# A phase mixer and a ternary FFN on one core: VectorE and ScalarE get new orders, and all steps are written out

## Chip, core and metric

The kernel runs on one core of one Trainium2 chip. The metric is device time in microseconds (us), from one execution's start to its end; the median of several runs counts, lower is better. One further execution was recorded by the hardware profiler.

## The reference

The input x has 16 sequences of 1024 positions of 256 features, all float32. The layer adds two blocks to it, each behind a layer norm:

```python
x = x + mixer(layernorm(x)); x = x + ffn(layernorm(x))
# mixer(x):
phi = cumsum((x @ W_omega.T + b_omega) * exp(log_scale) / sqrt(position), axis=1)
cm_real, cm_imag = x * cos(phi), x * sin(phi)
mem_real, mem_imag = cumsum(cm_real) / position, cumsum(cm_imag) / position
ret_real = mem_real * cos(phi) + mem_imag * sin(phi)
ret_imag = mem_imag * cos(phi) - mem_real * sin(phi)
context = concatenate([cm_real, cm_imag, ret_real, ret_imag])          # 1024 wide
return x + gelu(layernorm(context) @ W1.T + b1) @ W2.T + b2            # 1024 -> 512 -> 256
# ffn(x): weights rounded to -1, 0, 1:
return relu(x @ Wq1.T + b1) @ Wq2.T + b2                               # 256 -> 1024 -> 256
```

## The kernel before

The 16,384 positions are cut into 32 chunks of 512, two to a sequence; a chunk's second half of the state (the running sums of phase and memory) comes from the chunk ahead of it in the same sequence. Inside, features lie on the 128 partitions: a tile of [128, 2, 512] is one chunk of 256 features, called a wide tile here; a half-wide one is [128, 512]. To keep float32 accuracy in float16 matmuls, each activation is split: ScalarE casts the high part (`ch`, `gh`, `rh`, `xh`), and VectorE subtracts it from the whole for the low part (`cl`, `gl`, `rl`, `xl`).

The work is a software pipeline written by hand. Each engine has a function `step(s)`, which lists its operations for several chunks at once: `now` (chunk s, in its FFN), `nxt` (s+1, in the mixer's W1, Gelu and W2), `ahead` (s+2, in sine, cosine, running sums and retrieval), `far` (s+3, in the first norm and the phases). Engines run their lists strictly in order, and meet at semaphores: `need(engine, semaphore, chunk)` waits until that chunk's operation is done, and the last argument of `then_inc` names what an operation reports.

TensorE's step (not changed) is: `hidden` 0 and 1 (24 matmuls each, line 817), the statistics of the context (790, 796), `hidden` 2, `spread` of the context's reciprocal deviation `crs` (803), `hidden` 3, then `ffn_in` 0 to 7 (832) with the bias rows (842) and `ffn_out` (848) three blocks behind, `mixer_out` (864, 867), `omega` (777) and the last three `ffn_out`. `ffn_out(m)` needs `relu_lo(m)` of VectorE; `ffn_in(m)` for m below 4 needs the PSUM bank that `scale_hidden(m)` frees; `ffn_in(0)` needs the transposed rows that SyncE's DMAs bring after `second_lo`.

VectorE (`dve`) does `scale_hidden` (line 1160), `memory_real` and `memory_imag` (1099, 1105, times 1/position), the scans (1054, 1078, 1086), `relu_lo` (1204), `gelu_lo` (1165), `context_lo` (1136), `second_lo` (1196), `mixer_residual` (1172), `phase_turns` (1046), `output` (1210) and the small norm statistics. ScalarE (`act`) does all casts and tables. GpSimd (`pool`), whose list is not changed, does in each step: `inverse_std_2`, `square_lo`, `inverse_std_1`, `inverse_std_context` (474, writes `crs`), `product_imag_sin` (509, writes `qa`) and `square_sums` (494 and 496). `square_sums` waits for `square_real`, for `square_imag` and for `context_lo` of part 3:

```python
                need(pool, sqr_done, c)
                need(pool, sqi_done, c)
                need(pool, cl_done[3], c)
                pool.tensor_tensor(sqr[:, :, :], sqr[:, :, :], turn[:, :, :], ALU.add).then_inc(q2_done, 1)
```

Steps -1 to 1 and 28 to 31 are written out; steps 2 to 27 run as a hardware loop of 13 turns with two steps each, on every engine.

## Time and profile before

| | us |
|---|---|
| median of 3 runs | 1623.66 (1623.33 to 1623.72) |
| profiled execution, its own time | 1623.21 |
| its span, first to last instruction | 1621.1 |
| TensorE busy / VectorE busy | 1530.3 / 1470.2 |
| ScalarE busy / GpSimd busy | 1241.1 / 348.0 |

The granted TensorE clock is 0.987 of full speed on average and full over the steady steps. Busy time is time in which an engine executes something; on TensorE the ends of matmuls are modelled, and neighbours overlap, so starts are the better reading there. On VectorE and ScalarE too an instruction starts up to 0.1 us before its predecessor's end. In the rows below PE is TensorE, DVE VectorE, ACT ScalarE, POOL GpSimd, SPq SyncE's queue; "idle before <-releaser" is the time an engine stood still ahead of the instruction and who let it go.

### The profile page before, as it was taken

The page shows a single profiled execution, that of the slowest core. Times are in us where ns is not written, and L with a number is a line of the kernel's source. Part 1 is how long each engine was busy: PE and PEld are TensorE (multiplying, and loading weights), DVE is VectorE, ACT ScalarE, POOL GpSimd, SP SyncE. Part 2 cuts the span into 40 slices and gives each one's busy share as a digit, 9 for nine tenths or more (in the row PEclk, how much of TensorE's full clock was granted, in tenths as well). Part 3 has the DMA queues.
Part 4 walks back from the last instruction along what each step waited for, and adds up shares of the span by engine and source line. Part 5 has one row for each costly group of instructions (what it writes and reads, how often), then busy time and mean ns, then how long its engine had stood idle before and what let it go on. Part 6 is the DMA issues. An engine that isn't in the chain of part 4 may idle for free.

```text
span 1621.1 us, 31250 instructions
## 1 busy us (share of the span) xinstructions
PE 1530.3 (94%) x11177; PEld 925.6 (57%) x11177; DVE 1470.2 (91%) x2448; ACT 1241.1 (77%) x1773; POOL 348.0 (21%) x235
## 2 busy tenths in 40 slices
PE   3689999999999999999999999999999999999995
PEld 2455556566555665655566565556665555656553
DVE  7999999999999999999999999999999999999843
ACT  6678877787887787787777788777778777877843
POOL 1221222121122212212222211222221222222110
PEclk9899999999999999999999999999999999999998
DMA  5001111100111101111110111111001111010011
GB/s 201 14 14 27 40 40 40 36 16 26 39 39 39 39 24 28 26 39 39 39 39 13 26 39 39 39 39 36 16 26 39 39 39 39 23 28 15 27 27 39
DMA packets 109079, 57.95 MB, mean 36 GB/s; under 512 B 73456, under 2 KB 107504, under 8 KB 109040
## 3 DMA queue, kind: packets, MB, share of 16 engines
q1 hardware_dynamic: 107408, 53.77, 11.7%
q10 hardware_dynamic: 1632, 3.67, 0.6%
q8 instruction: 23, 0.38, 0.1%
q14 instruction: 16, 0.13, 0.0%
HBM read 23.87 MB, written 16.78 MB: 25 GB/s over the span
## 4 chain that ended last, share of the span: by engine, by line
DVE 42%; ACT 26%; issue 24%; PE 3%; POOL 3%; DVEq 1%; ACTq 1%; DMA 0%; SPq 0%; POOLq 0%
ACT arena L624 8%; ACT arena L599 6%; DVE ph L1054 5%; DVE mr L1086 5%; DVE mi L1078 4%; ACT arena L633 4%; DVE arena L1136 4%; DVE ph L1046 3%; DVE bn L1179 2%; DVE cmi L1071 2%; DVE xl L1038 2%; DVE rows L1196 2%; DVE x L1172 2%; DVE cmr L1069 2%; ACT xf L614 2%
## 5 line engine op out<-in xcount | busy, mean ns | idle before, releaser
L817 PE MATMUL ps<-arena,w_hi 128*128 128x512 f16 x2048 | 609.0, 379 | 2.9 <-DVE arena L1136 1.7
L817 PE MATMUL ps<-arena,w_lo 128*128 128x512 f16 x1024 | 388.0, 379 | 0.0
L817 PEld LDWEIGHTS ps<-arena,w_hi 128*128 128x128 f16 x2048 | 197.8, 98 | 223.7 <-issue 2.1
L848 PE MATMUL ps<-fw_t,arena 128*128 128x256 f16 x2048 | 254.6, 272 | 17.0 <-DVE arena L1204 16.0
L832 PE MATMUL ps<-turned,fw_t 128*128 128x512 f16 x1024 | 253.5, 381 | 13.0 <-DMA turned<-rows 13.0
L848 PEld LDWEIGHTS ps<-fw_t,arena 128*128 128x128 f16 x2048 | 191.5, 97 | 92.9 <-issue 58.0
L494 POOL TENSOR_TENSOR sqr<-sqr,turn 128x1024 f32<-128x1024 f32 x32 | 75.4, 2357 | 677.5 <-DVE arena L1136 677.5
L1204 DVE TENSOR_TENSOR arena<-arena 128x512 f16<-128x512 f32 x256 | 172.2, 683 | 41.6 <-ACT arena L633 41.4
L624 ACT ACTIVATE arena<-ps,relu_bias,relu_scale 128x512 f32<-128x512 f32 x256 | 194.1, 770 | 13.4 <-PE ps L832 13.3
L867 PE MATMUL ps<-w_hi,arena 128*128 128x256 f16 x1024 | 183.4, 273 | 0.0
L817 PEld LDWEIGHTS ps<-arena,w_lo 128*128 128x128 f16 x1024 | 100.1, 98 | 120.9
L585 ACT CAST sqr<-sqr 128x512 f16<-128x512 f32 x32 | 19.8, 618 | 188.4 <-POOL sqr L496 188.4
L832 PEld LDWEIGHTS ps<-turned,fw_t 128*128 128x128 f16 x1024 | 100.5, 98 | 101.3 <-DMA turned<-rows 13.3
L633 ACT CAST arena<-arena 128x512 f16<-128x512 f32 x256 | 153.3, 611 | 0.0
L867 PE MATMUL ps<-w_lo,arena 128*128 128x256 f16 x512 | 139.6, 273 | 0.0
L599 ACT ACTIVATE arena<-arena,b_full,z_down 128x512 f32<-128x512 f32 x128 | 103.5, 809 | 27.3 <-DVE arena L1160 27.3
L867 PEld LDWEIGHTS ps<-w_hi,arena 128*128 128x128 f16 x1024 | 100.2, 98 | 11.6
L509 POOL TENSOR_TENSOR qa<-mi,sn 128x1024 f32<-128x1024 f32 x32 | 76.5, 2390 | 100.7 <-DVE mi L1105 100.7
L603 ACT ACTIVATE arena<-arena,up 128x512 f16<-128x512 f32 x128 | 92.5, 722 | 4.2
L1165 DVE SCALAR_TENSOR_TENSOR arena<-arena,up 128x512 f16<-128x512 f32 x128 | 92.2, 741 | 0.0
L1160 DVE TENSOR_TENSOR arena<-ps,rb 128x512 f32<-128x512 f32 x128 | 81.8, 680 | 8.8 <-ACT rb L595 5.5
L474 POOL TENSOR_TENSOR crs<-cve,minus_half 128x4 f32<-128x4 f32 x32 | 33.3, 1040 | 228.0 <-DVE cve L1153 228.0
(190 smaller groups left out, 2739.7 us busy)
## 6 DMA issues: line engine op xcount, KB each, us to landing
x_rows<-in_L_attn_x SPq DMA_DIRECT2D x32, 512.0 KB, 3.5
out<-x SPq DMA_DIRECT2D x32, 512.0 KB, 2.9
arena<-in_L_attn_W ACTq DMA_DIRECT2D x1, 2048.0 KB, 11.2
arena<-in_L_ffn_W SPq DMA_DIRECT2D x2, 1024.0 KB, 10.4
turned<-rows SPq DMA_TRANSPOSE x128, 2.4
arena<-in_L_attn_ln_gamma ACTq DMA_DIRECT2D x1, 512.0 KB, 6.5
pos_rsqrt<-in_positions SPq DMA_DIRECT2D x1, 512.0 KB, 15.1
arena<-in_L_attn_ln_beta ACTq DMA_DIRECT2D x1, 512.0 KB, 12.7
```

Source lines behind the costliest of these rows:

```text
L599: act.activation(z[:, m], z[:, m], ACT.Gelu, scale=z_down[:, 0:1], bias=b1_full[:, m:m + 1])\
L603: act.activation(gh[:, m], z[:, m], ACT.Copy, scale=up[:, 3:4]).then_inc(gh_done[m], 1)
L624: act.activation(rf[:, m % SLOTS], ps[:, 4 + m % KE], ACT.Relu, scale=relu_scale[:, 0:1], bias=relu_bias[:, m:m + 1]).then_inc(relu_done[m ...
L633: act.copy(rh[:, m % SLOTS], rf[:, m % SLOTS]).then_inc(rh_done[m % SLOTS], 1)
L817: last = pe.matmul(ps[:, 4 + m], w[:, k, m * P:(m + 1) * P], a[:, c.b, k], start=(i == 0), stop=(i == len(passes) - 1))
L832: last = pe.matmul(ps[:, 4 + m % KE], fw1_t[:, k, m * P:(m + 1) * P], a[:, k], start=(i == 0), stop=(i == len(passes) - 1))
L848: last = pe.matmul(ps_rows_a[:, j], a[:, m % SLOTS, j * P:(j + 1) * P], fw2_t[:, m], start=False, stop=(m == KF - 1 and a is rl), skip_gro ...
L867: last = pe.matmul(ps_rows_b[:, j], a[:, m, j * P:(j + 1) * P], w[:, m], start=False, stop=(i == len(passes) - 1))
L1054: last = dve.tensor_tensor_scan(ph[:, k], ones[:, 0:1].to_broadcast([P, CH]), ph[:, k], ph_carry[:, k] if c.b else 0.0, ALU.mult, ALU.add)
L1160: dve.tensor_tensor(z[:, m], ps[:, 4 + m], rb[:, :], ALU.mult).then_inc(z_done[m], 1)
L1165: dve.scalar_tensor_tensor(out=gl[:, m], in0=z[:, m], scalar=up[:, 3:4], in1=gh[:, m], op0=ALU.mult, op1=ALU.subtract).then_inc(gl_done[m], 1)
L1204: dve.tensor_tensor(rl[:, m % SLOTS], rf[:, m % SLOTS], rh[:, m % SLOTS], ALU.subtract)\
```

## The change

Two things change. The loop is gone: `run` now lists all 33 steps on every engine. And the lists of VectorE and ScalarE are in a new order, for which some helper functions are cut in two (`sin_cos` into `sine` and `cosine`, `modulate` into its parts, `gelu` and `first_out` into a function and its cast); the carries of the running sums are copied only in a sequence's first chunk. `phase_sums` stands at the end of a step for `far` where it stood at the start of the next for `ahead`. The lists of TensorE, GpSimd and SyncE keep their order. The diff, cut to its core:

```diff
-            for s in range(first, LOOP_FROM):
-                step(Step(Counts(eng, s - s % 2), s % 2))
-            with eng.Fori(LOOP_FROM // 2, LOOP_TO // 2) as pair:
-                counts = Counts(eng, pair * 2)
-                step(Step(counts, 0))
-                step(Step(counts, 1))
-            for s in range(LOOP_TO, CHUNKS):
+            for s in range(first, CHUNKS):
                 step(Step(Counts(eng, s - s % 2), s % 2))
...
 
             def step(s):
                 now, nxt, ahead, far = s.chunk(0), s.chunk(1), s.chunk(2), s.chunk(3)
+                if nxt:
+                    sums_hi(nxt)
                 if ahead:
-                    act.activation(idle_sine[:, :], half_pi[:, 0:1], ACT.Sin)
                     whole_turns(ahead)
+                    base_scaled(ahead)
+                    sine(ahead)
                 if now:
                     normalise_2(now)
                 if ahead:
-                    sin_cos(ahead)
+                    cosine(ahead)
...
@@ -650,40 +652,63 @@
                 if now:
                     second_hi(now)
                 if ahead:
-                    base_scaled(ahead)
+                    context_hi(ahead, 1, cmi_done, cmi[:, :, :])
                     context_hi(ahead, 0, cmr_done, cmr[:, :, :])
...
                 if nxt:
                     spread_out(nxt)
                     gelu(nxt, 0)
                     gelu(nxt, 1)
...
-                    if m == 6 and ahead:
-                        square_imag(ahead)
-                if now:
-                    relu_hi(now, KF - 1)
+                if now:
+                    relu_hi(now, 0)
+                    relu(now, 1)
+                    relu(now, 2)
+                    relu_hi(now, 1)
+                    relu_hi(now, 2)
+                if nxt and now:
+                    gelu(nxt, 3)
+                if now:
+                    relu(now, 3)
+                    relu_hi(now, 3)
+                if nxt and now:
+                    gelu_hi(nxt, 3)
+                if now:
+                    relu(now, 4)
+                    relu(now, 5)
+                    relu_hi(now, 4)
+                if far:
+                    first_turned(far)
+                if now:
+                    relu_hi(now, 5)
+                    relu(now, 6)
+                if far:
+                    first_hi(far)
+                if now:
+                    relu(now, 7)
                 if ahead:
+                    square_imag(ahead)
                     context_hi(ahead, 2, rr_done, rr[:, :, :])
                     context_hi(ahead, 3, ri_done, ri[:, :, :])
-                    sums_hi(ahead)
+                if now:
+                    relu_hi(now, 6)
+                    relu_hi(now, 7)
+                if ahead:
+                    square_real(ahead)
+                if far:
+                    act.activation(idle_sine[:, :], half_pi[:, 0:1], ACT.Sin)
 
...
-            def carries(c):
-                need(dve, sumi_done, c)
-                dve.tensor_copy(mi_carry[:, :, :], mi[:, :, CH - 1:CH]).then_inc(icarry_done, 1)
+                if not c.b:
+                    need(dve, sumr_done, c)
+                    dve.tensor_copy(mr_carry[:, :, :], mr[:, :, CH - 1:CH]).then_inc(rcarry_done, 2)
+
...
             def step(s):
                 before, now, nxt, ahead, far = s.chunk(-1), s.chunk(0), s.chunk(1), s.chunk(2), s.chunk(3)
-                if ahead:
-                    phase_sums(ahead)
                 if now:
                     lean_2(now)
                 if before:
@@ -1226,63 +1263,73 @@
                     bias_pieces()
                     dve.wait_ge(p_fw1, 16)
                     signs(0, fw1_in, fw1_signs)
+                if ahead:
+                    modulate_imag(ahead)
+                    sums_imag(ahead)
+                    modulate_real(ahead)
+                    memory_imag(ahead)
                 if far:
                     gains_1(far)
-                if ahead:
-                    modulate(ahead)
-                if now:
-                    second_lo(now)
-                if ahead:
-                    sums_imag(ahead)
                 if nxt:
                     context_variance(nxt)
                 if far:
                     unit_squares(far)
+                if now:
+                    second_lo(now)
                 if ahead:
                     sums_real(ahead)
-                    carries(ahead)
-                    memory_imag(ahead)
                 if nxt:
...
                 if ahead:
                     memory_real(ahead)
+                    retrieve_imag_cos(ahead)
+                    retrieve_real_cos(ahead)
                 if nxt:
                     scale_hidden(nxt, 3)
-                if ahead:
-                    retrieve_real_cos(ahead)
-                    retrieve_imag_cos(ahead)
-                    product_real_sin(ahead)
...
                 if ahead:
+                    retrieve(ahead)
+                if now:
+                    relu_lo(now, 0)
+                if ahead:
+                    product_real_sin(ahead)
+                if now:
+                    relu_lo(now, 1)
+                    relu_lo(now, 2)
+                if nxt and now:
+                    gelu_lo(nxt, 0)
+                if ahead:
+                    context_lo(ahead, 0, cmr[:, :, :])
+                if nxt and now:
+                    gelu_lo(nxt, 1)
+                if now:
+                    relu_lo(now, 3)
+                if nxt and now:
+                    gelu_lo(nxt, 2)
+                if now:
+                    relu_lo(now, 4)
+                if nxt and now:
+                    gelu_lo(nxt, 3)
+                if ahead:
+                    retrieve_imag(ahead)
+                if now:
+                    relu_lo(now, 5)
+                if far:
+                    first_lo(far)
+                if ahead:
+                    context_lo(ahead, 1, cmi[:, :, :])
                     context_lo(ahead, 2, rr[:, :, :])
                     context_lo(ahead, 3, ri[:, :, :])
+                if now:
+                    relu_lo(now, 6)
+                    relu_lo(now, 7)
                 if nxt and not now:
                     dve.wait_ge(p_turned, FW1_TURNED)
                 if nxt:
@@ -1292,6 +1339,8 @@
                 if nxt:
                     statistics_2(nxt)
                     spread_2(nxt)
+                if far:
+                    phase_sums(far)
 
```

VectorE around the variance of the context, first before, then in the changed kernel: from `cve`, the last row of the variance, on. `sq` belongs to `unit_squares`, `rows` is `second_lo`, `arena<-ps,rb` is `scale_hidden`.

```order
L1153 TENSOR_SCALAR cve<-cvar 128x4
L1030 SCALAR_TENSOR_TENSOR sq<-rs,mv 128x4
L1033 TENSOR_TENSOR sq<-sq,rs 128x4
L1086 SCALAR_TENSOR_TENSOR mr<-ones,mr_carry,cmr 128x512 x2
L1092 COPY mi_carry<-mi 128x2
L1094 COPY mr_carry<-mr 128x2
L1105 TENSOR_TENSOR mi<-mi,pos_inv 128x1024
L1160 TENSOR_TENSOR arena<-ps,rb 128x512 x3
L1099 TENSOR_TENSOR mr<-mr,pos_inv 128x1024
```

The same place in the changed kernel:

```order
L1192 TENSOR_SCALAR cve<-cvar 128x4
L1058 SCALAR_TENSOR_TENSOR sq<-rs,mv 128x4
L1061 TENSOR_TENSOR sq<-sq,rs 128x4
L1235 TENSOR_TENSOR rows<-xs,rows 128x4x256
L1125 SCALAR_TENSOR_TENSOR mr<-ones,mr_carry,cmr 128x512 x2
L1199 TENSOR_TENSOR arena<-ps,rb 128x512 x3
L1137 TENSOR_TENSOR mr<-mr,pos_inv 128x1024
```

`second_lo` (`rows`) now follows the variance instead of preceding it, and the imaginary memory product and the two copies have left the place between the real scan and `scale_hidden`.

VectorE at the end of a step, from `relu_lo(5)` on, before and in the changed kernel. `arena<-arena` is `relu_lo`; `arena` from `cmi`, `rr`, `ri` is `context_lo` of parts 1 to 3; `x` is `mixer_residual`, `ph<-ps` is `phase_turns`.

```order
L1204 TENSOR_TENSOR arena<-arena 128x512
L1038 TENSOR_TENSOR xl<-xf,xh 128x1024
L1136 TENSOR_TENSOR arena<-cmi,arena 128x1024
L1204 TENSOR_TENSOR arena<-arena 128x512 x2
L1136 TENSOR_TENSOR arena<-rr,arena 128x1024
L1136 TENSOR_TENSOR arena<-ri,arena 128x1024
L1172 SCALAR_TENSOR_TENSOR x<-ps,h_down,base 128x1024
L1046 SCALAR_TENSOR_TENSOR ph<-ps,om_bias,pos_rsqrt 128x512 x2
```

The end of a VectorE step in the changed kernel:

```order
L1243 TENSOR_TENSOR arena<-arena 128x512
L1066 TENSOR_TENSOR xl<-xf,xh 128x1024
L1175 TENSOR_TENSOR arena<-cmi,arena 128x1024
L1175 TENSOR_TENSOR arena<-rr,arena 128x1024
L1175 TENSOR_TENSOR arena<-ri,arena 128x1024
L1243 TENSOR_TENSOR arena<-arena 128x512 x2
L1211 SCALAR_TENSOR_TENSOR x<-ps,h_down,base 128x1024
L1074 SCALAR_TENSOR_TENSOR ph<-ps,om_bias,pos_rsqrt 128x512 x2
```

`relu_lo(6)` and `relu_lo(7)` moved from ahead of `context_lo` of part 2 to behind that of part 3.

ScalarE in the second half of a step, before and in the changed kernel. `sqr<-mr` is `square_real`, `turn<-mi` is `square_imag`, `arena` from `ps` is `relu`, the half-wide casts are `relu_hi`.

```order
L581 ACTIVATE sqr<-mr 128x1024
L624 ACTIVATE arena<-ps,relu_bias,relu_scale 128x512
L633 CAST arena<-arena 128x512
L614 COPY xf<-ps 128x1024
L616 CAST xh<-xf 128x1024
L624 ACTIVATE arena<-ps,relu_bias,relu_scale 128x512
L633 CAST arena<-arena 128x512
L590 ACTIVATE turn<-mi 128x1024
L624 ACTIVATE arena<-ps,relu_bias,relu_scale 128x512
L633 CAST arena<-arena 128x512 x2
L576 CAST arena<-rr 128x1024
L576 CAST arena<-ri 128x1024
```

The same half of ScalarE's step in the changed kernel, from `relu(6)` on:

```order
L623 ACTIVATE arena<-ps,relu_bias,relu_scale 128x512
L615 CAST xh<-xf 128x1024
L623 ACTIVATE arena<-ps,relu_bias,relu_scale 128x512
L585 ACTIVATE turn<-mi 128x1024
L571 CAST arena<-rr 128x1024
L571 CAST arena<-ri 128x1024
L632 CAST arena<-arena 128x512 x2
L576 ACTIVATE sqr<-mr 128x1024
L711 ACT_TABLE_LOAD
L711 ACTIVATE idle_sine<-half_pi 128x1
L580 CAST sqr<-sqr 128x512
```

`square_real` moved from the first third of this stretch to its end, behind all casts of the FFN, and `sums_hi` (`sqr<-sqr`) stands behind the idle sine.

## Rows read from the trace of the kernel before

**Rows 1.** The page's first part: busy time, share of the span, instructions
```profile
PE 1530.3 (94%) x11177; PEld 925.6 (57%) x11177; DVE 1470.2 (91%) x2448; ACT 1241.1 (77%) x1773; POOL 348.0 (21%) x235
```

**Rows 2.** The chain that ended last: start, length, what
```profile
736.28 2.47 DVE ph L1054 x2
...
831.70 2.47 DVE ph L1054 x2
```

**Rows 3.** Timeline of TensorE, two steps: start, length, operation, idle before it
```profile
705.32 0.65 PE L803 MATMUL ps<-ident,crs 128*128 128x128 f32 x4 [0.63 <-POOL crs L474]
...
715.31 0.60 PE L842 MATMUL ps<-bias_row,ones_h 128*128 128x256 bf16 x4
716.37 1.03 PE L848 MATMUL ps<-fw_t,arena 128*128 128x256 f16 x8 [0.46 <-DVE arena L1204]
...
732.65 2.78 PE L848 MATMUL ps<-fw_t,arena 128*128 128x256 f16 x24
...
762.55 0.60 PE L842 MATMUL ps<-bias_row,ones_h 128*128 128x256 bf16 x4
```

**Rows 4.** Timeline of VectorE, the same stretch
```profile
706.88 1.23 DVE L1105 TENSOR_TENSOR mi<-mi,pos_inv 128x1024 f32<-128x1024 f32 x1
...
709.81 1.81 DVE L1099 TENSOR_TENSOR mr<-mr,pos_inv 128x1024 f32<-128x1024 f32 x1
...
725.42 0.69 DVE L1204 TENSOR_TENSOR arena<-arena 128x512 f16<-128x512 f32 x1 [0.68 <-ACT arena L633]
...
730.64 1.22 DVE L1136 TENSOR_TENSOR arena<-ri,arena 128x1024 f16<-128x1024 f32 x1
...
744.51 0.16 DVE L1021 SCALAR_TENSOR_TENSOR lean<-rs,mv 128x4 f32<-128x4 f32 x1 [1.12 <-POOL rs L465]
```

**Rows 5.** Table of waits: us in total, times, longest
```profile
DVE ph L1054 <- issue: 13.4, 13, 1.1
```

**Rows 6.** Timeline of GpSimd, the same stretch
```profile
708.18 2.36 POOL L509 TENSOR_TENSOR qa<-mi,sn 128x1024 f32<-128x1024 f32 x1 [2.92 <-DVE mi L1105]
732.03 2.36 POOL L494 TENSOR_TENSOR sqr<-sqr,turn 128x1024 f32<-128x1024 f32 x1 [21.49 <-DVE arena L1136]
...
751.46 1.01 POOL L474 TENSOR_TENSOR crs<-cve,minus_half 128x4 f32<-128x4 f32 x1 [6.98 <-DVE cve L1153]
```

**Rows 7.** Timeline of GpSimd, prologue
```profile
47.84 3.26 POOL L509 TENSOR_TENSOR qa<-mi,sn 128x1024 f32<-128x1024 f32 x1 [9.56 <-DVE mi L1105]
65.63 2.35 POOL L494 TENSOR_TENSOR sqr<-sqr,turn 128x1024 f32<-128x1024 f32 x1 [14.53 <-DVE arena L1136]
68.06 2.07 POOL L496 TENSOR_TENSOR sqr<-sqr 128x512 f32<-128x512 f32 x1
```

**Rows 8.** Timeline of VectorE, prologue
```profile
47.68 1.22 DVE L1099 TENSOR_TENSOR mr<-mr,pos_inv 128x1024 f32<-128x1024 f32 x1
48.93 3.25 DVE L1121 TENSOR_TENSOR rr<-mr,cs 128x1024 f32<-128x1024 f32 x1
...
67.02 4.18 DVE L1054 TENSOR_TENSOR_SCAN ph<-ones,ph_carry,ph 128x512 f32<-128x512 f32 x2 [0.24 <-DVE ph L1046]
```

**Rows 9.** Groups by line: times counted, busy us, mean ns of one
```profile
L624 ACT ACTIVATE arena<-ps,relu_bias,relu_scale 128x512 f32<-128x512 f32 x256 | 194.1, 770 | 13.4 <-PE ps L832 13.3
...
L1204 DVE TENSOR_TENSOR arena<-arena 128x512 f16<-128x512 f32 x256 | 172.2, 683 | 41.6 <-ACT arena L633 41.4
L633 ACT CAST arena<-arena 128x512 f16<-128x512 f32 x256 | 153.3, 611 | 0.0
...
L599 ACT ACTIVATE arena<-arena,b_full,z_down 128x512 f32<-128x512 f32 x128 | 103.5, 809 | 27.3 <-DVE arena L1160 27.3
...
L603 ACT ACTIVATE arena<-arena,up 128x512 f16<-128x512 f32 x128 | 92.5, 722 | 4.2
...
L576 ACT CAST arena<-ri 128x1024 f16<-128x1024 f32 x32 | 33.5, 1047 | 0.0
```

**Rows 10.** Timeline of SyncE, the same stretch
```profile
748.62 5.14 SPq L443 DMA_TRANSPOSE turned<-rows  x4
```

98 lines of the change are left out of this document (45 added, 53 removed).

## The prediction

> **What bounds the kernel now.** First I read the shares of the page: TensorE is busy 94% of the span and VectorE 91% [rows 1], so a few tenths of a microsecond per step on either decide. Then the chain that ended last: the same scan comes back every 95.42 us, two steps of 512 positions, 47.71 each [rows 2]. Then TensorE's own timeline [rows 3]. From one FFN bias group (line 842) to the next it takes 47.24 us. Behind the four bias matmuls the first `ffn_out` starts 1.06 us after the group's start, where 0.44 would do (an estimate: four matmuls of 256 columns, eight of which take 0.87 in step time in the same timeline), so 0.62 is lost waiting for `relu_lo(0)` on VectorE. In every second step, the one behind a loop turn, the context spread (line 803) waits 0.63 more for GpSimd's `crs`. Last, VectorE's timeline of the same stretch [rows 4]: it idles 1.12 for GpSimd's reciprocal root (line 1021), 0.68 for a ScalarE cast (line 1204), and, in the table of waits, 13.4 in 13 turns of the loop (line 1054, "issue") [rows 5]. So VectorE's list is what TensorE waits for, and VectorE works about 45.3 us of a 47.24 us step (47.24, less 1.12 and 0.68, less some 0.1 that each restart costs).
>
> One more reading carries the forecast. `mi*pos_inv` and `mr*pos_inv` are the same operation on the same shape, yet take 1.23 and 1.81 us, in all 32 steps [rows 4]. The second runs while GpSimd multiplies `qa` (708.18 to 710.54) [rows 6]. The prologue shows it bare: GpSimd's `qa` is asked at 47.84 while `mr*pos_inv` runs, takes 3.26 instead of 2.36, and the VectorE product behind it takes 3.25 instead of 1.21 [rows 7, 8]. The scan at 67.02 starts inside GpSimd's add (65.63 to 67.98); the next GpSimd add takes 2.07, and two scans that need 2.47 take 4.18 [rows 2, 7, 8]. So a VectorE operation with two SBUF inputs and a GpSimd tensor operation exclude each other for their whole length, and GpSimd gets its turn at the end of the running VectorE instruction, even where the next one stands ready. Operations that read PSUM are untouched: the `scale_hidden` ones beside `qa` and line 1172 beside the add keep their time. In the kernel before, `qa` starts with three `scale_hidden` and the add of squares (732.03 [rows 6]) starts as `mixer_residual` does, so nearly all of both is hidden.
>
> The Trainium skill (SBUF — State Buffer, section "SBUF: two separate sides") says so too: VectorE and GpSimd share a port pair as an exclusive lock for a whole instruction, and a VectorE operation with two SBUF inputs counts. The rows above agree with it, and it speaks against this change. At a full 2.36 us for each of the two collisions below, a step would be 49.3 us by that page, an estimate.
>
> **The change part by part.**
> *Loop written out.* It takes away VectorE's turn, 13.4 us in 13 pairs of steps [rows 5], 1.03 each. Six of the steps are straight-line already and have no such wait, so that fetching more code shows no price; I take 0 and, as bound, the 1 us per step that a turn costs now.
> *Reordering on VectorE that removes waits.* `gains_1` now comes after `sums_imag`, so 1.12 is covered by 6 us of other work; the 0.68 goes because the cast it waited for is issued earlier. `context_variance` ahead of `second_lo` gives GpSimd's `crs` in time, so 0.63 goes. Carries are copied in every second chunk only: about 0.3 us saved there, and 0.15 us of new back-to-back dependence (`modulate_imag` to its scan). The cosine now ends about 0.25 us after VectorE wants it (ScalarE does `base_scaled` 2.0, sine, `normalise_2` 2.0 and the absolute value ahead of it). The phase scan stands behind the same `spread_2` as before; only its place in the code moved, worth 0.
> *The turned operands.* `second_lo` moves some 3.3 us back relative to TensorE's step, behind scan, product and variance. The four transposes after it take 5.14 to issue [rows 10], the last one lands 2.4 after its issue by the page, together about 6.5; they then land about when `ffn_in(0)` wants them. I take 0, up to 0.5 a step.
> Summed in the new order, VectorE's list without exclusion is 44.5 us: 45.3, less 0.58 because `mr*pos_inv` no longer meets `qa`, less 0.3 for copies, plus 0.1 net of dependence and cosine.
> *First collision.* GpSimd's own order is unchanged: `crs`, then `qa`. Its `crs` [rows 6] starts right behind the variance and ends 1.09 us after it; `qa` is asked 0.07 later, in the last part of `second_lo` (which starts 0.38 after the variance and takes 1.22). GpSimd gets the port when `second_lo` ends, and the scan `sums_real` behind it stands for 2.36 less the overlap of 0.2. Cost 2.15 a step; bounds 2.04 (line 1121: 3.25 less 1.21) and 2.36. Nothing excludes it: whichever instruction boundary GpSimd gets, scan or scan follows, and `scale_hidden` comes only afterwards.
> *Second collision.* `relu_lo(6)` and `relu_lo(7)` now stand between `context_lo(3)` and `mixer_residual`. They take two SBUF operands. GpSimd's add of squares is released by `context_lo(3)` and by `square_real`, which moved to the end of ScalarE's list. Both are counted from the end of `scale_hidden(0)`. VectorE up to the end of `context_lo(3)`: 3 `scale_hidden`, 4 `gelu_lo`, 6 `relu_lo` and 11 wide operations, 1.8 + 2.65 + 3.6 + 12.5 = 20.55 us (each row's length less 0.08, since neighbours overlap [rows 4, 9]). ScalarE up to the end of `square_real`: 4 Gelu, 4 upcasts, 8 ReLU, 8 casts, 6 wide: 2.83 + 2.5 + 5.3 + 4.05 + 5.8 (each length less 0.1 [rows 9]), with 0.1 for waits: 20.6. GpSimd asks about 0.1 later, at 20.7. `relu_lo(6)` gives up the port at about 20.97 (start 20.46, 0.68 long, handed over some 0.18 before its end as in [rows 7, 8]). So GpSimd wins over `relu_lo(7)` by 0.25 us and holds it for 2.36, which delays `mixer_residual` and `phase_turns` by 2.15. Bounds: 0, if ScalarE is more than 0.25 later than counted, and 2.36. I take 2.15, as the nearest count has it.
> *Sum.* 44.5 + 2.15 + 2.15 = 48.8 in odd chunks, 49.0 in even ones with the copies: 48.9 us a step. VectorE then never waits for TensorE, and TensorE, which would do a step in 46.6 (47.24 less 0.62), waits 2.3. Against 47.71 that is +1.2. The 28 full steps between the first and the 29th take 28 x 1.2 = 34 more. The head gains one to three us of collisions in the first steps (+2), the last three steps, where VectorE is light, lose their waits (-1.5). Span 1621.1 + 34.5 = 1655.6. The profiled execution reported 1623.21 beside its span of 1621.1, the median of the runs is 1623.66, 2.6 over the span: 1658.
>
> **The rivals.**
> *One collision only* (ScalarE 0.25 us slower in those 30 instructions, or GpSimd asked after `relu_lo(7)` began). For it: the margin is a hundredth of the sums it comes from, and Gelu after Gelu stands nowhere in the trace. Then `relu_lo(0)` is ready 30.8 us after `phase_turns` began (the new order's list up to there with 2.15 in it), TensorE needs 16.3 from there to the end of omega (716.37 to 732.65) [rows 3], 0.2 more for `relu_lo(3)`: 47.3 to 47.4 a step, 28 times 0.35 less than now, -10, the ends -0.5: 1621.1 - 10.5 + 2.6 = 1613.
> *No exclusion counts* (the GpSimd operations slip between, or the scan's broadcast operand frees it). Then TensorE bounds the step at its 46.6: 28 x 1.1 = 31 less, 3 more at the ends, 1621.1 - 34 + 2.6 = 1590. Against it: 32 of 32 products at 1.81 and the two prologue cases. This is also what the change would bring if only its waits were counted.
> *Worse than forecast.* The transposes, late already, add their 0.5 where VectorE is late too, or GpSimd's other operations meet products: 49.4 and more, over 1670.
> The first rival is the one on the other side of no change, and the 0.25 us of margin decide between it and the forecast. That the change does nothing is hardly possible with both lists rewritten.
>
> **How the numbers follow.** Two collisions 0.58, one 0.27, none 0.08, worse 0.07. Predicted is the first, its own range 1648 to 1668. The range leaves out "none" and "worse": 1607 to 1668. Faster by over 0.2% (3.2 us, about what runs of this kernel can tell) holds one and none, 0.32 with a little of the first rival falling into no change; same 0.05; slower 0.63.
>
> **What would show it.** `mr*pos_inv` falls to 1.23. The first `sums_real` scan of each pair lasts about 3.3 instead of 1.2: if it stays at 1.2, the reading of the exclusion is wrong. `relu_lo` groups with one of 2.8 among them show the second collision; GpSimd's add starting after `relu_lo(7)` refutes it. VectorE's waits at lines of `gains_1` and at the scan vanish. TensorE idles over 2 us a step ahead of `ffn_in(0)`, the first `ffn_out` or both. Wrong it would be if ScalarE's chain ends later, or if the port goes to the waiting VectorE instruction.

## Result and the profile after

The change makes the kernel 0.3% faster: 1618.73 us (median of 8 runs, 1617.69 to 1619.34) against 1623.6 (8 runs beside them), ratio 0.9969, 95% interval 0.9958 to 0.998. Forecast were 1658 and, as range, 1607 to 1668. The direction was wrong, the time lies in the range only because the range spans the rival with one collision, and that rival (1613) was nearest. The profiled execution took 1619.34 with a span of 1617.5; the granted TensorE clock is 0.987, as before.

The page's first part, the groups of GpSimd's two wide operations, and four rows of the table of waits (total, times, longest):

```profile
PE 1533.0 (95%) x11177; PEld 925.9 (57%) x11177; DVE 1510.8 (93%) x2400; ACT 1232.9 (76%) x1773; POOL 416.4 (26%) x235
```
```profile
L486 POOL TENSOR_TENSOR sqr<-sqr,turn 128x1024 f32<-128x1024 f32 x32 | 99.5, 3108 | 747.8 <-ACT sqr L576 711.7 <-DVE arena L1175 36.0
L501 POOL TENSOR_TENSOR qa<-mi,sn 128x1024 f32<-128x1024 f32 x32 | 83.3, 2602 | 9.8 <-DVE mi L1144 9.8
```
```profile
PEld ps L860 <- DMA turned<-rows: 21.4, 10, 13.3
...
PEld ps L860 <- DVE arena L1199: 18.5, 27, 1.1
DVE ph L1074 <- PE ps L805: 18.0, 29, 0.7
...
PE ps L876 <- DVE arena L1243: 9.9, 28, 0.4
```

Against [rows 1] VectorE is busy 41 us more with 48 instructions fewer, and GpSimd 68 more with the same 235: their operations did not grow in number, they grew in length. The 13.4 us of loop turns of [rows 5] and the two VectorE waits of [rows 4] (0.68, 1.12) are gone. The add of squares took 2.36 in every steady step [rows 6] and takes 3.11 on average now.

One steady step, VectorE first (start, length; x2 is two instructions), then GpSimd, ScalarE, TensorE:

```profile
1082.75 1.21 DVE L1235 TENSOR_TENSOR rows<-xs,rows 128x1024 f16<-128x1024 f32 x1
1083.89 4.48 DVE L1125 TENSOR_TENSOR_SCAN mr<-ones,cmr 128x512 f32<-128x512 f32 x2
...
1090.41 1.21 DVE L1137 TENSOR_TENSOR mr<-mr,pos_inv 128x1024 f32<-128x1024 f32 x1
...
1108.62 1.22 DVE L1175 TENSOR_TENSOR arena<-ri,arena 128x1024 f16<-128x1024 f32 x1
1109.76 1.29 DVE L1243 TENSOR_TENSOR arena<-arena 128x512 f16<-128x512 f32 x2
1110.96 1.28 DVE L1211 SCALAR_TENSOR_TENSOR x<-ps,h_down,base 128x1024 f32<-128x1024 f32 x1
```
```profile
1083.60 2.57 POOL L501 TENSOR_TENSOR qa<-mi,sn 128x1024 f32<-128x1024 f32 x1
1110.06 3.20 POOL L486 TENSOR_TENSOR sqr<-sqr,turn 128x1024 f32<-128x1024 f32 x1 [23.89 <-ACT sqr L576]
```
```profile
1108.91 1.07 ACT L576 ACTIVATE sqr<-mr 128x1024 f32<-128x1024 f32 x1
```
```profile
1094.55 1.04 PE L860 MATMUL ps<-turned,fw_t 128*128 128x512 f16 x4 [0.30 <-DVE arena L1199]
1095.43 0.60 PE L870 MATMUL ps<-bias_row,ones_h 128*128 128x256 bf16 x4
1096.38 1.03 PE L876 MATMUL ps<-fw_t,arena 128*128 128x256 f16 x8 [0.35 <-DVE arena L1243]
```

The first collision is here as forecast: GpSimd asks for `qa` at 1083.60, within `second_lo`, gets the port (the way to SBUF that it shares with VectorE) when that ends, and the two scans take 4.48 where they took 2.33 to 2.45 in the kernel before. `mr*pos_inv` is back at 1.21 (1.81 in [rows 4]). The second is not: GpSimd asks for the add at 1110.06, 0.30 into `relu_lo(6)` and 0.30 ahead of `relu_lo(7)`, so it asks before (7) starts, and yet the pair takes 1.29, as two free ones do. It is GpSimd that waits, until (7) is through: 3.20 is 2.36 and 0.84. It was so in 27 of the 32 chunks; in the others GpSimd asked after (7) had begun, or the prologue and end have another order. TensorE waits for `scale_hidden` in 27 steps and for `relu_lo(0)` in 28, VectorE for TensorE's omega in 29: the two hold each other in one circle, into which the 2.1 us of the scans go (the kernel without these 2.1, e2_gate, bears this out). Steps take as a rule 47.28 and 47.66 us in turn, from one bias group (line 870) to the next, 47.47 on average, against 47.24 and 48.18 of before; with the irregular ones among them the 28 steps from the first group on average 47.54, against 47.67.

### The profile page after: what moved, and what is told of

It reads as the page before. It is cut to its first block, busy times and chain, and to the rows that moved or that the text cites. A ratio compares the mean times of both kernels' runs of the same rounds, so it can differ in the third digit from the quotient of the medians.

```text
span 1617.5 us, 30589 instructions
## 1 busy us (share of the span) xinstructions
PE 1533.0 (95%) x11177; PEld 925.9 (57%) x11177; DVE 1510.8 (93%) x2400; ACT 1232.9 (76%) x1773; POOL 416.4 (26%) x235
## 4 chain that ended last, share of the span: by engine, by line
PE 50%; DVE 31%; issue 12%; ACT 3%; DMA 1%; SPq 1%; DVEq 0%; POOL 0%; ACTq 0%; POOLq 0%
PE ps L845 13%; PE ps L876 11%; PE ps L895 10%; PE ps L860 8%; DVE mr L1125 5%; PE ps L805 5%; DVE arena L1199 3%; DVE ph L1083 2%; DVE mi L1113 2%; DVE rr L1160 2%; DVE mr L1137 2%; DVE mi L1144 1%; DVE bn L1218 1%; PE ps L818 1%; DVE rows L1235 1%
## 5 line engine op out<-in xcount | busy, mean ns | idle before, releaser
L486 POOL TENSOR_TENSOR sqr<-sqr,turn 128x1024 f32<-128x1024 f32 x32 | 99.5, 3108 | 747.8 <-ACT sqr L576 711.7
L860 PE MATMUL ps<-turned,fw_t 128*128 128x512 f16 x1024 | 258.4, 382 | 22.4 <-DMA turned<-rows 16.9
L860 PEld LDWEIGHTS ps<-turned,fw_t 128*128 128x128 f16 x1024 | 97.6, 98 | 119.6 <-DMA turned<-rows 21.4
L553 ACT ACTIVATE turn<-ph,rounder 128x1024 f32<-128x1024 f32 x32 | 36.8, 1150 | 100.3 <-DVE ph L1083 100.3
L895 PEld LDWEIGHTS ps<-w_hi,arena 128*128 128x128 f16 x1024 | 100.1, 98 | 11.6
L501 POOL TENSOR_TENSOR qa<-mi,sn 128x1024 f32<-128x1024 f32 x32 | 83.3, 2602 | 9.8 <-DVE mi L1144 9.8
## 6 DMA issues: line engine op xcount, KB each, us to landing
arena<-in_L_ffn_W SPq DMA_DIRECT2D x2, 1024.0 KB, 11.6
arena<-in_L_attn_ln_beta ACTq DMA_DIRECT2D x1, 512.0 KB, 13.4
```

Source lines behind the costliest of these rows:

```text
L860: last = pe.matmul(ps[:, 4 + m % KE], fw1_t[:, k, m * P:(m + 1) * P], a[:, k], start=(i == 0), stop=(i == len(passes) - 1))
L895: last = pe.matmul(ps_rows_b[:, j], a[:, m, j * P:(j + 1) * P], w[:, m], start=False, stop=(i == len(passes) - 1))
```

## The experiments

Eighteen kernels, in the order in which they ran; "changed" is the changed kernel. Each stands against runs of the kernel before that were taken beside it (medians 1623.2 to 1625.5 us). The edits are shown shortened: a line in words stands for the lines that it names. Eight of the kernels (e6, e9, e11, e12, e13, e15, e17, e18) leave the whole layer out and hold only trials of the handover, so that their total time says nothing; they, e14_seven and e16_break have one run each.

**1 to 4: which part gives and which takes.** Four edits: the kernel before without its loop; the changed kernel with the product held back; with square and subtractions moved together; with the loop put back.

```diff
 e1_flat (kernel before)
-            with eng.Fori(LOOP_FROM // 2, LOOP_TO // 2) as pair:
+            for s in range(first, CHUNKS):
 e2_gate (changed), product_imag_sin
                 need(pool, mi_done, c)
+                need(pool, sumr_done, c)
 e3_three (changed), ScalarE and VectorE
+                square_real(ahead)                 # ahead of relu_hi 6 and 7
+                relu_lo(now, 5); relu_lo(now, 6); relu_lo(now, 7)    # all behind context_lo 3
 e4_loop (changed)
+            with eng.Fori(LOOP_FROM // 2, LOOP_TO // 2) as pair:     # new orders in the old loop
```

> The kernel before with its loop written out and both orders kept. Theory 1 (a turn of the loop costs VectorE 1.05 us and that puts the context spread 0.8 us late, once in two steps): 13 turns at 0.9 to 1.05 us less, 1623.6 - 12 to 13.5 = 1610 to 1612, and the wait of TensorE for GpSimd's root at the context spread is gone. If so, the new orders by themselves cost about 7 us. Rival (the gain of the change comes from the orders, the loop turn is absorbed elsewhere): 1621 to 1624. The transposes land 6.5 us after the low part and have 3 us to spare here, so late landings cost nothing.

> The changed kernel, with one wait more on GpSimd: its product of the imaginary memory and the sine also waits until the real scan is done, so that it runs beside the scale_hidden operations, which read PSUM. Theory 1 (exclusion of the port is what holds the step at 47.47 us): the real scans take 2.4 instead of 4.45 us, the product mr*pos_inv rises from 1.21 to 1.8, VectorE gains 1.5 us a step, TensorE's matmuls bound the step at 46.5 to 46.7: 1618.7 - 28 x 0.85 = 1591 to 1597. Rival (the scan is long but VectorE has room, TensorE's waits come from the late transposes): no change, 1616 to 1620; or, if the late product delays the retrieval, slower.

> The changed kernel with square_real issued ahead of relu_hi 6 and 7, so that GpSimd's add of squares is asked 0.17 us after context_lo of part 3, and with three relu_lo (5, 6, 7) behind that part instead of two. It asks who gets the port between back-to-back half-wide subtractions. Theory E (a race at the edge: GpSimd must ask more than 0.3 us before the next VectorE instruction starts): GpSimd asks 0.35 before relu_lo 6 and 0.95 before relu_lo 7, gets the port at one of the two boundaries, and one relu_lo lasts 2.8 to 3; a step costs 1.3 to 2.1 us more, 1655 to 1680. Theory R (a run of short instructions keeps the port until it ends): GpSimd's add lasts 3.7 to 3.9 us instead of 3.2, no relu_lo is longer than 0.7, time as the changed kernel, 1617 to 1621.

> The changed kernel's orders inside the old hardware loop (steps 2 to 27 in 13 turns). Theory 1 (each turn costs VectorE about 1 us, of which TensorE sees 0.7 to 1): 1618.7 + 9 to 13, less 3 to 4 us of transposes that land late beside instruction fetches in the written-out form: 1624 to 1629. Rival (writing out gains nothing by itself here since VectorE waits 0.6 us for omega in each step): 1614 to 1619.

| kernel | median us | ratio to before, 95% |
|---|---|---|
| e1_flat | 1611.3 | 0.9921 (0.9907 to 0.9934) |
| e2_gate | 1586.72 | 0.9772 (0.9759 to 0.9786) |
| e3_three | 1701.55 | 1.0479 (1.0463 to 1.0495) |
| e4_loop | 1635.13 | 1.0071 (1.0057 to 1.0084) |

Writing the steps out gives 12.4 us by itself; the new orders by themselves cost 11.5 in the loop and 7.4 without it. e2_gate adds one wait to GpSimd and takes 32 us off the changed kernel, 4 us more than the best that was expected: 23 of the 28 steady steps take 46.43 us, and in these TensorE's timeline shows no wait. Its `qa` now runs beside `scale_hidden`, and the scans are at 2.45:

```profile
1108.12 2.45 DVE L1126 TENSOR_TENSOR_SCAN mr<-ones,mr_carry,cmr 128x512 f32<-128x512 f32 x2
...
1112.40 1.75 DVE L1138 TENSOR_TENSOR mr<-mr,pos_inv 128x1024 f32<-128x1024 f32 x1
```
```profile
1110.71 2.36 POOL L502 TENSOR_TENSOR qa<-mi,sn 128x1024 f32<-128x1024 f32 x1 [2.84 <-DVE mr L1126]
```

e3_three is 22 us slower than the worst that was expected: GpSimd gets the port ahead of `relu_lo(6)` for the add and ahead of (7) for the next add as well, and three subtractions that need 1.9 us take 5.11:

```profile
558.47 5.11 DVE L1243 TENSOR_TENSOR arena<-arena 128x512 f16<-128x512 f32 x3
```
```profile
558.72 2.64 POOL L486 TENSOR_TENSOR sqr<-sqr,turn 128x1024 f32<-128x1024 f32 x1 [23.43 <-DVE arena L1175]
561.44 1.60 POOL L488 TENSOR_TENSOR sqr<-sqr 128x512 f32<-128x512 f32 x1
```

e4_loop is 6 us above its expected range, since the turn costs more than in the kernel before: a pair of steps takes 96.31 us against 94.95 written out. VectorE stands 1.06 at the turn, `second_lo` is that much later, and the transposes behind it have no slack left in the new order:

```profile
1082.10 0.16 DVE L1050 SCALAR_TENSOR_TENSOR lean<-rs,mv 128x4 f32<-128x4 f32 x1 [1.06 <-issue]
```
```profile
1101.74 1.90 PE L868 MATMUL ps<-turned,fw_t 128*128 128x512 f16 x8 [1.05 <-DMA turned<-rows]
```

**5 to 8: is it the moment of the request?** e5_sqr moves only `square_real` ahead of `relu_hi` 6 and 7. e6_port is the handover alone. e7_turn is e2_gate with `second_lo` first; e8_gate2 is e3_three with the add held back:

```diff
 e7_turn, VectorE
+                if now: second_lo(now)
                 if far: gains_1(far)
                 if nxt: context_variance(nxt)
                 if far: unit_squares(far)
-                if now: second_lo(now)
 e8_gate2, GpSimd
                     product_imag_sin(ahead)
+                    need_block(pool, rl_done, KF - 1, now)
                     square_sums(ahead)
 e6_port, one trial
+    VectorE:  relu_lo; first; victim                # back to back
+    ScalarE:  copy of 300 + 15 t columns            # its end releases GpSimd
+    GpSimd:   qa = mi * sn
```

> The changed kernel with one move on ScalarE: square_real is issued ahead of relu_hi 6 and 7 instead of behind them. GpSimd's add of squares then waits for VectorE's last context_lo instead of for ScalarE's square, and asks for the port 0.25 us after relu_lo(6) has started, where in the changed kernel it asks 0.30 us after. Theory E (a request that is made early enough within relu_lo(6) gets the port ahead of relu_lo(7), and 0.05 us decides; the run with three relu_lo had 0.25 us and GpSimd won): relu_lo(7) lasts 2.84 us instead of 0.68, the add 2.64 instead of 3.20, the step grows by 1.5 to 2.2 us, and the time is 1665 to 1688 us. Rival F (GpSimd won there because three relu_lo stood in a row, or because more work was late, not because of the moment of the request): relu_lo(7) stays at 0.68 us and the time at 1617 to 1621 us.

> No part of the layer is computed: the outputs are filled with a constant, and the kernel holds only 192 trials of the handover. In each, VectorE runs three operations back to back (a relu_lo, then a first operation, then a victim), ScalarE a copy whose length grows by 15 columns (about 12 ns) from trial to trial, and GpSimd asks for the port with the product of qa when that copy ends. Four pairs of 48 trials: relu_lo then relu_lo, second_lo then scan, second_lo then relu_lo, relu_lo then scan. Theory E (an edge in time): in each pair the victim is long (about 2.8 us for relu_lo, 3.4 us for the scan) for every request before one moment, and short for every later one; for relu_lo the edge lies between 0.25 and 0.30 us after the start of a relu_lo, that is between 0.35 and 0.30 us ahead of the victim. Theory V (the edge is set by the victim: a scan claims the port later than a subtraction does): the edge ahead of a scan is under 0.29 us in both its pairs, and 0.30 to 0.35 us ahead of relu_lo in both of its. Theory P (the edge is set by the operation before): the two pairs behind second_lo have one edge, the two behind relu_lo another. Theory L (length of wait): no clean edge.

> The changed kernel with GpSimd's product held until sums_real is done (as in the run that took 1586.7 us) and, besides, second_lo issued ahead of gains_1, context_variance and unit_squares, 1.1 to 1.2 us earlier on VectorE. Theory T (what is left above 46.43 us a step are the transposes that land late, 7.1 to 7.5 us behind second_lo in 4 or 5 steps of the 28, where TensorE asks 6.6 to 6.7 us behind it): those steps lose their 0.4 to 0.9 us each, all steady steps are 46.43 us, and the time falls by 2 to 4 us, to 1582.5 to 1585. Rival R (the variance is now 1.1 us late, and through GpSimd's root and the spread it holds scale_hidden): the steps grow by up to 1.1 us, and the time is 1600 to 1622 us. Rival 0: no measurable difference, 1586 to 1587.5.

> The run with three relu_lo behind the last context_lo and square_real early (1701.6 us), and with one wait more: GpSimd's add of squares waits until relu_lo(7) is done. Nothing else is moved. Theory E (all that the earlier run lost to the changed kernel, 83 us or 2.6 us a step, was the port: relu_lo(6) at 2.84 and relu_lo(7) at 1.75 us where each takes 0.6): both are back at 0.6 to 0.7 us, and the time is that of the changed kernel, 1616 to 1626 us. Rival (the order itself costs, since relu_lo(5) is late for TensorE and square_real holds relu_hi): a loss of 10 to 50 us against the changed kernel stays, 1630 to 1670 us.

e5_sqr took 1621.74 us (ratio 0.9989, 0.998 to 0.9998). In 27 chunks GpSimd asked 0.25 us into `relu_lo(6)`, as early as it had into the subtraction ahead of the loser in e3_three, and did not win: the add lasts 3.25, `relu_lo(7)` 0.68. My theory that a few hundredths of a microsecond in the moment of the request decide falls. In two chunks it did win, and each time VectorE had restarted 0.05 us late just ahead of `relu_lo(6)`, where it has no gap in the 27 others:

```profile
872.63 3.45 DVE L1243 TENSOR_TENSOR arena<-arena 128x512 f16<-128x512 f32 x2
```
```profile
872.75 2.78 POOL L486 TENSOR_TENSOR sqr<-sqr,turn 128x1024 f32<-128x1024 f32 x1 [23.71 <-DVE arena L1175]
```

These two losses of 2.16 us each are about what e5_sqr took more than the changed kernel (3.0), and the gap is what the later experiments come to. e8_gate2 took 1618.91 (0.9972, 0.9962 to 0.9982), the changed kernel's time: all 83 us that e3_three had lost were the port, and the order of the subtractions is worth nothing. e7_turn took 1585.06 (0.9766, 0.9753 to 0.978), the best version here, 38 us under the kernel before: 26 of the 28 steady steps are at 46.43 us, since TensorE asks for the turned rows 7.8 us after `second_lo` and no longer 6.6, while they land after 6.3 as a rule, after 7.1 to 7.4 in four chunks, and after 8.2 and 7.2 in two near the end.

In e6_port the victim is the operation that stands next in VectorE's list, and b the one that runs ahead of it. In all trials but the very first (in which ScalarE started late and the request came behind the victim) GpSimd got the port at the end of the instruction that was running: relu_lo 2.83 instead of 0.68 us, a scan 3.36 instead of 1.20. The sweep reaches down to 0.10 us ahead of the victim. The few requests around b's own start show how late is late enough: 0.028 us ahead of it GpSimd still wins over b, 0.017 ahead it has to wait for b's end. So in isolation the forecast's rule holds and in the changed kernel it does not.

**9 to 14: two theories that fell.** In the changed kernel VectorE takes up the waits for operations further on while `relu_lo(6)` runs. e9_waits puts waits ahead of b (the running operation) and the victim; e10_early and e14_seven move waits in the changed kernel; e11_third and e12_third let the operation behind the victim be released at a swept moment; e13_chain puts up to two operations ahead of b.

```diff
 e10_early, VectorE
                 context_lo(ahead, 2, rr[:, :, :])
+                waits of relu_lo 6 and 7
                 context_lo(ahead, 3, ri[:, :, :])
-                waits of relu_lo 6
                 relu_lo 6
-                waits of relu_lo 7
                 relu_lo 7
 e14_seven, VectorE
                 context_lo(ahead, 3, ri[:, :, :])
+                waits of relu_lo 7
                 waits of relu_lo 6
                 relu_lo 6
-                waits of relu_lo 7
                 relu_lo 7
```

> Again no part of the layer is computed and the outputs are a constant. 192 trials of three relu_lo back to back (first, b, victim), with GpSimd's request moved by about 17 ns from trial to trial, in six groups of 32 that differ in the semaphore waits that VectorE has ahead of b and of the victim; every wait but the sixth group's is for a value that was reached long before. Groups: waits ahead of b and victim 0 and 1; 0 and 2; 0 and 3; 2 and 2; 3 and 3; and, last, no wait ahead of b and a wait for b's own end ahead of the victim. In the trials of before, without any wait, GpSimd won every request made up to 0.10 us ahead of the victim. Theory W (relu_lo(7) kept the port in the changed kernel because VectorE took up its wait only 0.08 us ahead of its start, so that nothing was queued when the port came free): in the groups in which a wait instruction is recorded within 0.1 us ahead of the victim, the victim stays at 0.68 us for requests made 0.20 to 0.36 us ahead of it, and is about 2.83 us where no wait instruction stands so near. Rival A (waits have no part in it): the victim is 2.83 us in every group, for every request from 0.10 to 0.60 us ahead. Rival B (the wait has to be for something that arrives late): only the sixth group shows short victims.

> The changed kernel, with the waits of relu_lo(6) and relu_lo(7) taken up ahead of the last context_lo instead of directly ahead of each; no operation is moved. In the changed kernel VectorE's wait instruction was recorded 0.08 us ahead of relu_lo(7), and GpSimd, which had asked 0.21 to 0.31 us ahead of it, did not get the port. Theory W (a wait taken up that late is what kept the port for relu_lo(7)): now no wait stands between relu_lo(6) and relu_lo(7), GpSimd gets the port, relu_lo(7) lasts 2.84 us, the add 2.6, and the time is 1665 to 1690 us. Rival A (it was something else): relu_lo(7) stays at 0.68 us and the time is 1616 to 1622 us.

> No part of the layer is computed and the outputs are a constant. 192 trials: VectorE runs three relu_lo back to back (first, b, victim) and then a third operation that waits for a second, short copy of ScalarE; GpSimd asks at the end of ScalarE's first copy, some 0.23 us ahead of that. The two move together by about 5 ns from trial to trial, GpSimd's request from 0.16 to 0.39 us after b's start and the end of the third operation's wait from about 0.38 to 0.61 us. Four groups of 48: third operation as mixer_residual with PSUM input, waiting; the same without the late wait; a relu_lo as the third, waiting; as the first group, and behind it one more relu_lo with three waits. Theory D (what let relu_lo(7) keep the port in the changed kernel is that the operation behind it was released, by w2_done, 0.47 to 0.49 us after b's start, just ahead of the handover at 0.53; in 28 of 29 and 27 of 27 steps with that moment GpSimd lost, and with any other moment, 0.43 and 0.56 us among them, it won): in the groups that wait, the victim is 0.68 us long for the trials in which the wait ends 0.47 to 0.49 us after b's start, and 2.83 us in the others; in the second group it is 2.83 us throughout. Rival (the moment of w2_done has no part): 2.83 us in all 192, and what decides there stays open.

> No part of the layer is computed and the outputs are a constant. The trials of the run before with ScalarE's second copy lengthened from 8 to 180 columns, since the end of the third operation's wait had come only 0.03 us behind GpSimd's request and had swept 0.19 to 0.42 us after b's start, and not the 0.47 to 0.49 of the changed kernel (in all its 192 trials but the first GpSimd won). Now the wait should end some 0.17 us behind the request, as in the changed kernel, and sweep 0.33 to 0.56 us after b's start. Groups of 48: third operation with PSUM input and one wait; with three waits; a relu_lo with one wait; three waits and one more relu_lo behind. Theory D (a release of the third operation 0.04 to 0.06 us ahead of the handover keeps the port for the victim): the victim is 0.68 us long where the wait ends 0.47 to 0.49 us after b's start, 2.83 us elsewhere, at least in the groups with three waits, which are the changed kernel's pattern. Rival: 2.83 us in all trials; then the moment of the release isn't enough, and what decides stays open.

> No part of the layer is computed and the outputs are a constant. 192 trials of VectorE operations back to back, GpSimd's request moved by 10 ns from trial to trial over b's 0.6 us; in four groups of 48 the run ahead of b differs: two context_lo, then b, then the victim, then an operation from PSUM; the same with the last held back by a late wait; two relu_lo ahead of b; one context_lo ahead of b. (b and the victim are relu_lo throughout.) Theory C (after two or more operations in an unbroken run ahead of b, VectorE keeps the port between b and the victim): the victim stays at 0.68 us in the first three groups at requests 0.2 to 0.4 us after b's start, and is 2.83 us in the fourth. Rival: 2.83 us in all four; then the run ahead has no part in it.

> The changed kernel with the waits of relu_lo(7) alone taken up early, ahead of relu_lo(6) instead of ahead of relu_lo(7), so that the operations run as unbroken as in the changed kernel and no wait stands between the two. If the wait ahead of relu_lo(7) keeps the port for it, GpSimd now wins: relu_lo(7) 2.84 us long, 1675 to 1690 us. Theory C (the unbroken run of operations ahead of relu_lo(6), which the run with both waits moved had broken, keeps the port): relu_lo(7) stays at 0.68 us and the time at 1616 to 1622 us.

In the trials GpSimd won in every group of e9, e11, e12 and e13, the first trial of a kernel apart (in five of e9's it came early enough to win over b already); in e11 the release came too early by my own slip (0.19 to 0.42 us after b's start), which e12 mended (0.33 to 0.56). In such short runs waits and the release of a later operation have no part in it. But e10_early, which moves no operation, took 1681.92 us (1.0358, 1.034 to 1.0377), and e14_seven 1620.09 in a single run, with `relu_lo(7)` at 0.68. What sets them apart is a gap: in e10_early VectorE stands 0.52 us ahead of the last `context_lo`, in nearly every chunk, and in e14_seven it does not.

```profile
553.12 1.23 DVE L1175 TENSOR_TENSOR arena<-ri,arena 128x1024 f16<-128x1024 f32 x1 [0.52 <-ACT arena L632]
554.26 3.44 DVE L1249 TENSOR_TENSOR arena<-arena 128x512 f16<-128x512 f32 x2
```

In the changed kernel VectorE has no gap from 1088.61 up to `relu_lo(7)`; each instruction starts 0.07 to 0.08 us before its predecessor's end, and the last nineteen ahead of it all have two SBUF inputs. In e3_three there is a gap at 556.19, three operations ahead of the first one that lost.

**15 to 18: the length of the run.** A run here is a row of VectorE's operations without a gap between them. e16_break is the changed kernel with one gap. The three others are the isolated trials with longer runs (C is `context_lo`, r, b and v are `relu_lo`, R is `second_lo`, s a scan; behind the victim v or s comes an operation from PSUM).

```diff
 e16_break, VectorE
+                need(dve, cl_done[2], ahead)       # its own operation just before
                 context_lo(ahead, 3, ri[:, :, :])
 e15_long:    CCCCCC b v,  CCC b v,  CCCCCC R s,  rrrrrrrrrrrr b v
 e17_length:  CCCC b v,  CCCCC b v,  rrrr b v,  rrrrrr b v,  rrrrrrrr b v,  CCCCCC R v,  CCCCCC b s,  C rrrrrr b v
 e18_keep:    rrrrrrrr b, then v,  vv,  vvvv,  vvvvvvvv,  vvvv s
```

> No part of the layer is computed and the outputs are a constant. 192 trials in four groups of 48: six context_lo without a gap, then b and the victim (both relu_lo), then an operation from PSUM; three context_lo, b, victim; six context_lo, second_lo as b, and a scan as the victim; twelve relu_lo, b, victim. GpSimd's request moves by 10 ns (third group 7 ns) through b. Theory C (a long unbroken run of operations lets VectorE keep the port): in groups 1 and 4, perhaps 2, the victim stays at 0.68 us for requests 0.2 to 0.4 us after b's start; the third shows whether a scan behind such a run still loses, as in the changed kernel (3.36 us). Rival: every victim is lengthened by 2.15 us.

> The changed kernel with one wait more on VectorE: the last context_lo waits for the end of the one before it, a gap of about 0.12 us, and nothing is moved. Theory C (the unbroken run keeps the port; every case that GpSimd won had a gap one or two operations ahead of b): with this gap GpSimd gets the port, relu_lo(7) is 2.84 us long, and the time 1675 to 1690 us. Rival: relu_lo(7) stays at 0.68 us, and the time is 1617 to 1624 us (0.12 us a step more at most).

> No part of the layer is computed and the outputs are a constant. Eight groups of 24 trials; GpSimd's request moves by 13 ns from 0.15 us after b's start (0.75 us where b is second_lo). Ahead of b stand, without a gap: four context_lo; five; four relu_lo; six; eight; six context_lo with second_lo as b; six context_lo with a scan as the victim; and a context_lo with six relu_lo. If the number of operations counts (theory N), groups with the same number fall alike whatever their length: by the runs so far the change lies between 4 and 7 operations with b, so that four context_lo and four relu_lo agree, and eight relu_lo are certainly short. If the time since the gap counts (theory T), it lies between 3.4 and 6.8 us ahead of b: four and six relu_lo (2.4 and 3.6 us) are like three context_lo, the victim at 2.83 us. For the scan: if the victim decides (theory V), the group with a scan behind b is long (3.36 us) and the one with second_lo as b and relu_lo behind it short (0.68); if b decides, the other way round.

> No part of the layer is computed and the outputs are a constant. 120 trials: eight relu_lo and b without a gap, GpSimd's request moving by 13 ns through b, and behind b one, two, four or eight more relu_lo, or four and a scan, before the operation from PSUM. If VectorE keeps the port only for the next operation (theory 1), the second relu_lo behind b is 2.83 us long from the second group on, and GpSimd's product lasts 2.9 to 3.3 us in all groups. If it keeps it for as long as its run goes on (theory 2), no relu_lo is lengthened, and GpSimd's product lasts longer by 0.60 us for each relu_lo more, up to 7.5 us in the fourth group; in the fifth it gets the port ahead of the scan, which lasts 3.36 us.

e16_break took 1661.24 us in a single run, 42.5 more than the changed kernel. The wait makes the last `context_lo` start 0.11 us later (0.03 us behind its predecessor's end, where it had started 0.08 ahead of it), and `relu_lo(7)` lost the port in 26 chunks. The mechanism is the expected one; the time is 14 us under the expected range. In three more chunks GpSimd asked 0.01 to 0.02 us ahead of (7) and did not win, as in e6_port. One of the 26:

```profile
546.49 1.23 DVE L1175 TENSOR_TENSOR arena<-ri,arena 128x1024 f16<-128x1024 f32 x1
547.63 3.44 DVE L1243 TENSOR_TENSOR arena<-arena 128x512 f16<-128x512 f32 x2
```

Isolated, in e15_long (six `context_lo`, b and victim; the request at 313.90 falls within b) VectorE keeps the port and both subtractions are done in 1.29. In e17_length with one `context_lo` fewer (request at 314.19) they take 3.43. The first three rows are of e15_long, the last two of e17_length:

```profile
306.68 6.90 DVE L128 TENSOR_TENSOR cl<-mrs,ch 128x1024 f16<-128x1024 f32 x6 [1.14 <-SPq L85]
313.50 1.29 DVE L122 TENSOR_TENSOR rl<-rf,rh 128x512 f16<-128x512 f32 x2
```
```profile
313.90 3.09 POOL L98 TENSOR_TENSOR qa<-mi,sn 128x1024 f32<-128x1024 f32 x1 [7.34 <-ACT dst L108]
```
```profile
308.27 5.77 DVE L134 TENSOR_TENSOR cl<-mrs,ch 128x1024 f16<-128x1024 f32 x5
313.95 3.43 DVE L128 TENSOR_TENSOR rl<-rf,rh 128x512 f16<-128x512 f32 x2
```

| victim's place in the run (run ahead of b) | trials | GpSimd wins |
|---|---|---|
| 5th (CCC) | 48 | 48 |
| 6th (CCCC, rrrr) | 47 | 47 |
| 7th (CCCCC) | 24 | 24 |
| 8th (CCCCCC b v, CCCCCC R v, rrrrrr b v) | 95 | 0 |
| 9th or later (C rrrrrr, 8 r, 12 r) | 215 | 0 |
| 8th or later, the victim a scan | 96 | 96 |

The first trial of each kernel, whose request came too late, is not counted; in four of the 310 trials of the 8th and later places the request was less than 0.02 us ahead of the victim, too late to tell. The number decides and not the time: six `relu_lo` ahead of b last 3.6 us and protect the victim, five `context_lo` 5.7 us and do not. In e18_keep VectorE keeps the port for as long as the run goes on. Seventeen `relu_lo` take what they take alone, and GpSimd's product 7.46 instead of 2.36:

```profile
783.30 10.32 DVE L125 TENSOR_TENSOR rl<-rf,rh 128x512 f16<-128x512 f32 x17 [1.14 <-SPq L88]
```
```profile
788.38 7.46 POOL L101 TENSOR_TENSOR qa<-mi,sn 128x1024 f32<-128x1024 f32 x1 [5.20 <-ACT dst L111]
```

A scan behind such a run loses all the same: 3.36 us in all 24 of e18's fifth group, after four `relu_lo` that were not touched.

## Why the prediction was wrong

- **The step that failed** is "So GpSimd wins over `relu_lo(7)` by 0.25 us". Both moments in it were right, and not by luck: VectorE's 20.55 us from the end of `scale_hidden(0)` on were 20.54, ScalarE's 20.6 were 20.68. `square_real` ended at 1109.98, the request came at 1110.06, 0.30 us ahead of `relu_lo(7)`. The rule under it was not. "GpSimd gets its turn at the end of the running VectorE instruction, even where the next one stands ready" was read from prologue rows [rows 7, 8], where VectorE's runs are short. In all trials it holds up to the seventh operation behind a gap (and ahead of a scan always), and `relu_lo(7)` stands behind nineteen. What the runs showed in its place: VectorE keeps the port there, `relu_lo(7)` takes its 0.68 us and GpSimd waits 0.84, so that the second collision costs VectorE 0 and not 2.15 us a step. The bound 0 for this term had been put down to ScalarE being late, which it was not.
- **What the failed term is worth.** With the second collision in place the forecast's mechanism is real: 49.52 us a step and 1681.9 us in e10_early (its gap of 0.52 us is in this), 49.04 and 1661.2 in e16_break, against 48.9 and 1658 forecast.
- **The first collision** stands, in place, cause and size: 2.1 us on VectorE a step (4.48 and 4.54 for two scans, less 2.33 and 2.45), against 2.15 taken. Its reading had one slip: `mr*pos_inv` took 1.81 in 31 of the 32 chunks, and 1.22 in the prologue's first. Its price to the kernel is 32 us (e2_gate), 1.04 a step, since without it TensorE bounds the step at 46.43, near the 46.6 of the rival "no exclusion counts" (1590; e2_gate took 1586.7). That is no point for this rival, for the exclusion is there; e2_gate only moves it beside operations from PSUM.
- **The rival that came true** had 47.3 to 47.4 a step and 1613; measured are 47.47 and 1618.7. Over 28 steps 0.12 makes 3.4 us, and the irregular ones among them (47.54 on average in place of 47.47) 1.9 more; the ends, forecast 0.5 shorter, came out 0.3 longer. What makes steps irregular is mostly a transpose that lands late, and the term "The transposes" was taken as 0, up to 0.5 a step. As a rule they land 6.30 us after `second_lo`, just ahead of the 6.6 to 6.7 at which TensorE wants them, but in five chunks after 7.3 to 7.7, and `ffn_in(0)` starts 0.6 to 1.1 us late in each; three of the five fall into the 28 steps (of the 21.4 in the table of waits 13.3 are the last chunk's). Why these land late, the runs do not show. e7_turn, which asks 1.2 later, gets most of this back on top of e2_gate (1.7 us).
- **Loop.** 1.03 a pair and 13.4 in all were forecast; e1_flat gives 12.4. In the new orders the same turn costs 16.4 (e4_loop), since the transposes' slack is used up (TensorE wanted them 9.7 us after `second_lo` and they landed after 6.5; now it would want them after 5.5).
- **The waits** (0.68, 1.12, 0.63 for `crs`) went as said. But the 0.63 had been put down to the new order, and e1_flat, which keeps the old one, shows that it goes with the loop: TensorE waited 16 times for `crs`, 11.6 us in all, and 2 times, 2.6 us, in e1_flat. The phase scan's new place in the code was not tried by itself.

The Trainium skill (SBUF — State Buffer, section "SBUF: two separate sides") has VectorE and GpSimd exclude each other for a whole instruction. The runs agree with it for each pair that met (3.25, 3.36, 2.83 us); which of the two goes first decided between 1619 and 1682 us here.

## What to carry to other kernels

A GpSimd tensor operation that is released just ahead of a VectorE scan, or of one of the first seven two-input operations behind a gap, puts nearly its whole length on VectorE (2.15 of 2.36 us here). Hold it back with a wait until VectorE reads PSUM: one such wait was worth 32 us here, more than all of the change. Count the operations behind the last gap before you price a collision, and expect that a new gap of 0.1 us can cost 1.6 us a step (e16_break); the rows of a prologue, where VectorE's runs are short, misled here about a long unbroken run. When an order uses up the slack of a transfer, price the late landings and not the usual one.
